# Seeding a PSUM bank by ScalarE in a Strassen-Winograd loop, and copying running sums out in place of VectorE's adds

## The reference

```
y   = x @ W.T + 2 * sum_e gate1[e] * (x @ A[e].T) @ B[e].T      gate1: softmax of the two largest of 8 biased logits
z   = y @ Wf.T + b + 2 * sum_e gate2[e] * (y @ Af[e].T) @ Bm[e]  gate2: softmax over 4 experts
out = x + z
```

## Time and profile before

| | |
|---|---|
| runs | 322.85, 323.37, 323.40 us; median 323.37 |
| profiled execution | span 321.9 us from the first to the last instruction |
| median less that span | 1.5 us |
| TensorE, matmul | 318.2 us busy (99%), 2246 matmuls |
| VectorE | 262.5 us (82%), 609 instructions |
| ScalarE | 128.2 us (40%), 258 instructions |
| GpSimd | 11.3 us (3%) |
| DMA | 27.59 MB |
| granted TensorE clock | 1.000 |

### The profile page before, as it was taken

The page is one execution under the profiler, slowest core; times in us unless marked ns, Lnnn a source line. Parts: engine busy times, 40 slices in busy tenths (PEclk is TensorE's granted clock), DMA queues, the critical chain, the costliest instruction groups (busy, mean ns, idle before and its releaser), DMA issues.

```text
span 321.9 us, 5996 instructions
## 1 busy us (share of the span) xinstructions
PE 318.2 (99%) x2246; PEld 311.9 (97%) x2246; DVE 262.5 (82%) x609; ACT 128.2 (40%) x258; POOL 11.3 (3%) x13
## 2 busy tenths in 40 slices
PE   8999999999999999999999999999999999999996
PEld 5999999999999899899999999999999999999996
DVE  3999999798799778988968968878895987888543
ACT  3872836495147236325412503421251350333111
POOL 1001003700000000000000000000000000000000
DMA  7999000000000312700330150051025006002003
GB/s 266 419 404 290 3 2 0 2 0 2 0 2 0 132 24 46 260 3 0 109 154 1 60 201 0 0 191 70 0 74 187 0 21 239 0 0 110 24 0 130
DMA packets 10704, 27.59 MB, mean 86 GB/s; under 512 B 3166, under 2 KB 4702, under 8 KB 10688
## 3 DMA queue, kind: packets, MB, share of 16 engines
q1 hardware_dynamic: 10256, 26.83, 23.5%
q10 hardware_dynamic: 432, 0.53, 0.5%
HBM read 18.97 MB, written 8.39 MB: 85 GB/s over the span
## 4 chain that ended last, share of the span: by engine, by line
PE 98%; DMA 1%; DVE 0%; issue 0%
PE sums L1310 98%; DMA in<-part 1%; PE sums L1571 0%; DVE rows L1069 0%; DVE b_high L806 0%
## 5 line engine op out<-in xcount | busy, mean ns | idle before, releaser
L1310 PE MATMUL sums<-b_high,a_high 128*128 128x256 f32 (+1 forms) x224 | 45.3, 286 | 0.3 <-DVE b_high L806 0.3
L1310 PE MATMUL sums<-b_low,a_high 128*128 128x256 f32 (+1 forms) x224 | 45.2, 286 | 0.0
L1310 PE MATMUL sums<-b_high,a_low 128*128 128x256 f32 (+1 forms) x224 | 45.0, 286 | 0.0
L1310 PEld LDWEIGHTS sums<-b_high,a_high 128*128 128x128 f32 x224 | 34.7, 189 | 1.0 <-ACT a_high L549 0.8
L1310 PEld LDWEIGHTS sums<-b_low,a_high 128*128 128x128 f32 x224 | 34.7, 189 | 0.0
L1310 PEld LDWEIGHTS sums<-b_high,a_low 128*128 128x128 f32 x224 | 34.6, 188 | 0.0
L1310 PE MATMUL sums<-t_high,s_high 128*128 128x354 f32 x96 | 31.3, 326 | 0.0
L1310 PE MATMUL sums<-t_low,s_high 128*128 128x354 f32 x96 | 31.1, 324 | 0.0
L1310 PE MATMUL sums<-t_high,s_low 128*128 128x354 f32 x96 | 31.1, 324 | 0.0
L1069 DVE TENSOR_TENSOR rows<-sums,rows 128x354 f32<-128x354 f32 x48 | 24.4, 522 | 4.1 <-PE sums L1310 3.4
L1310 PE MATMUL sums<-ct_low,st_high 128*128 128x244 f32 (+1 forms) x80 | 25.6, 320 | 0.0
(11 more groups left out here) (151 smaller groups left out, 845.8 us busy)
## 6 DMA issues: line engine op xcount, KB each, us to landing
stage<-tokens SPq DMA_DIRECT2D x14, 512.0 KB, 4.0
out<-rows SPq DMA_DIRECT2D x14, 512.0 KB, 4.9
in<-part SPq DMA_DIRECT2D x7, 585.0 KB, 8.8
in<-part SPq DMA_DIRECT2D x4, 777.0 KB, 14.0
in<-part SPq DMA_DIRECT2D x4, 265.0 KB, 16.4
rows<-tokens SPq DMA_DIRECT2D x2, 512.0 KB, 13.6
out<-rows SPq DMA_DIRECT2D x3, 192.0 KB, 2.3
c_plain<-gate_proj SPq DMA_DIRECT2D x1, 544.0 KB, 18.0
```

The costliest lines, as they stand in the source:

```text
L1310: return nc.tensor.matmul(out_, lhs, rhs, start=start, stop=stop, skip_group_check=True)
```

## The change

In the loop rounds (pairs 2 to 6, `seeding` and `turning`), and only there:

- product 1 is no longer copied to SBUF. ScalarE waits until bank B is out (its own signal) and copies bank A into bank B (`b_seeded`). Product 6 does not open bank B but accumulates on that copy, and waits for `b_seeded`; product 2 waits for nothing of its own.
- since bank B now holds product 1 + product 6 (+ product 7 ...), U2, U3 and the final sum of bank B are plain ScalarE copies of the bank, in place of three VectorE adds. Each has a place in ScalarE's program: U2 behind the seed, U3 behind the second half of ut_high, the final one behind the copy of bank A.
- product 5 moves from behind product 7 to the place between products 1 and 6.
- pairs 0, 1 and 7 stay as they were, but for the constants that they wait for on `r1_read`, as this is no longer signalled in the loop, and a wait of VectorE for `u2_read` before its last add of bank C.

```diff
--- before.py
+++ after.py
@@ -318,6 +318,7 @@
         p6_done = sem("p6_done")
         p7_done = sem("p7_done")
         r1_read = sem("r1_read")
+        b_seeded = sem("b_seeded")
         u2_read = sem("u2_read")
         u3_read = sem("u3_read")
         r22_read = sem("r22_read")
@@ -696,6 +697,8 @@
 
             def pair(j, first=False, second=False, last=False):
                 steady = not first and not second
+
+                seeding = steady and not last
                 if not first:
                     round_next(j, S4, p3_done)
                 if second:
@@ -721,7 +724,15 @@
                 if not first:
                     act.wait_ge(stored[1], 16 * j)
                 act.wait_ge(p1_done, j + 1)
-                copy(rows[:, 1, wide_at(0)], bank(BANK_A)).then_inc(r1_read, 1)
+                if seeding:
+
+                    act.wait_ge(b_out, j)
+                    copy(bank(BANK_B), bank(BANK_A)).then_inc(b_seeded, 1)
+                    act.wait_ge(stored[0], 16 * j)
+                    act.wait_ge(p6_done, j + 1)
+                    copy(rows[:, 0, wide_at(1)], bank(BANK_B)).then_inc(u2_read, 1)
+                else:
+                    copy(rows[:, 1, wide_at(0)], bank(BANK_A)).then_inc(r1_read, 1)
                 if first:
                     act.wait_ge(t4_made, 1)
                     round_t(T4, C11)
@@ -739,6 +750,8 @@
                 act.wait_ge(u_turned, j + 1)
                 if steady and not last:
                     copy(half_of(ut_high, 1), ut_plain_half(1)).then_inc(ut_high_ready, 1)
+                    act.wait_ge(p7_done, j + 1)
+                    copy(rows[:, 1, wide_at(1)], bank(BANK_B)).then_inc(u3_read, 1)
                 else:
                     copy(ut_high[:, :, :], ut_psum).then_inc(ut_high_ready, 1)
                 if second:
@@ -774,6 +787,9 @@
                     act.wait_ge(stored[0], 16 * j)
                 act.wait_ge(a_done, j + 1)
                 copy(rows[:, 0, wide_at(0)], bank(BANK_A)).then_inc(a_out, 1)
+                if seeding:
+                    act.wait_ge(b_done, j + 1)
+                    copy(rows[:, 1, wide_at(0)], bank(BANK_B)).then_inc(b_out, 1)
                 if first:
                     round_next(j + 1, S2, p6_done)
                     round_next(j + 1, S3, p7_done)
@@ -1196,11 +1212,12 @@
                     add_sums(rows[:, 1, wide_at(1)], bank(BANK_C), rows[:, 1, wide_at(1)]).then_inc(r22_read, 1)
 
 
-                if not first:
-                    dve.wait_ge(stored[0], 16 * j)
-                dve.wait_ge(r1_read, j + 1)
-                dve.wait_ge(p6_done, j + 1)
-                add_sums(rows[:, 0, wide_at(1)], bank(BANK_B), rows[:, 1, wide_at(0)]).then_inc(u2_read, 1)
+                if not turning:
+                    if not first:
+                        dve.wait_ge(stored[0], 16 * j)
+                    dve.wait_ge(r1_read, j - 4 if last else j + 1)
+                    dve.wait_ge(p6_done, j + 1)
+                    add_sums(rows[:, 0, wide_at(1)], bank(BANK_B), rows[:, 1, wide_at(0)]).then_inc(u2_read, 1)
                 if turning:
                     turn_u(j)
 
@@ -1213,7 +1230,6 @@
                 else:
                     low_part(ut_low[:, :, :], ut_psum, ut_high[:, :, :]).then_inc(ut_low_ready, 1)
                 if turning:
-                    add_u3()
                     add_r22()
                 if first:
                     split_t(T4, C11)
@@ -1286,8 +1302,9 @@
                 dve.wait_ge(r22_read, j + 1)
                 dve.wait_ge(d_done, j + 1)
                 add_sums(rows[:, 1, wide_at(1)], bank(BANK_D), rows[:, 1, wide_at(1)]).then_inc(d_out, 1)
-                dve.wait_ge(b_done, j + 1)
-                add_sums(rows[:, 1, wide_at(0)], bank(BANK_B), rows[:, 1, wide_at(0)]).then_inc(b_out, 1)
+                if not turning:
+                    dve.wait_ge(b_done, j + 1)
+                    add_sums(rows[:, 1, wide_at(0)], bank(BANK_B), rows[:, 1, wide_at(0)]).then_inc(b_out, 1)
                 if turning:
                     split_s(j + 1, S3)
                 if not last:
@@ -1295,6 +1312,7 @@
                 if first:
                     split_s(j + 1, S2)
                     split_s(j + 1, S3)
+                dve.wait_ge(u2_read, j + 1)
                 dve.wait_ge(c_done, j + 1)
                 add_sums(rows[:, 0, wide_at(1)], bank(BANK_C), rows[:, 0, wide_at(1)]).then_inc(c_out, 1)
                 assert step[0] == STEPS, step
@@ -1558,10 +1576,15 @@
 
                 if first:
                     pe.wait_ge(t_split, T2 + 1)
+                if turning:
+                    product_5(j)
                 pe.wait_ge(s_split, 4 * j + s_no[S2])
-                if not first:
+                if turning:
+
+                    pe.wait_ge(b_seeded, j - 1)
+                elif not first:
                     pe.wait_ge(b_out, j)
-                of_s(BANK_B, S2, t_high[T2], t_low[T2], True).then_inc(p6_done, 1)
+                of_s(BANK_B, S2, t_high[T2], t_low[T2], not turning).then_inc(p6_done, 1)
                 if first:
                     product_5(j, first=True)
 
@@ -1580,7 +1603,8 @@
                 if not steady:
                     turn_u()
 
-                pe.wait_ge(r1_read, j + 1)
+                if not turning:
+                    pe.wait_ge(r1_read, j - 4 if last else j + 1)
                 if first:
                     pe.wait_ge(cw_split, B21 + 1)
                 of_x(BANK_A, 0, 1, cw_high[B21], cw_low[B21], False).then_inc(p2_done, 1)
@@ -1594,8 +1618,6 @@
                 pe.wait_ge(s_split, 4 * j + s_no[S3])
                 pe.wait_ge(u2_read, j + 1)
                 of_s(BANK_B, S3, t_high[T3], t_low[T3], False).then_inc(p7_done, 1)
-                if turning:
-                    product_5(j)
                 if steady:
                     small_y()
                 lora(BANK_A, 0, 0)
```

## The result

The changed kernel took 324.79 us (median of six runs, 323.89 to 325.18); the kernel before 323.31 us in the same comparison. The ratio is 1.0046, 95% interval 1.0032 to 1.0061: slower by 1.5 us, in an interval of 1.0 to 2.0. The forecast was 325.0 us.

A forecast was written before the change was run, and what follows sets the result against it. TensorE, busy 99%, was taken as the bound, so only its waits count. A stall of +1.9 us less 0.3 us coming back, on 323.37 us, gave 325.0 us; own range 324.4 to 325.9, toward other cases 323.6 to 326.4.

The forecast's parts named there:

- What bounds the kernel: Whole kernel: TensorE is busy 99% of 321.9 us, so only its waits count; ut_low before small_y has no slack.
- The order of the slots: Loop rounds: five product slots still end at 229.57, but product 2 moves one 1.95 us slot later.
- What hangs on product 2: Ahead of small_y: late product 2 delays round_x, ut_high, ut_low and the weight load; 0.38 us in five rounds, +1.9 us.
- Its size: Stall ahead of small_y's weight load: 0.36 to 0.39 us, taken as 0.38, in each of five rounds.
- The seed: ScalarE's copy into bank B before product 6: slack 0.7 us with the signal, product 5 as cover, cost nothing.
- The copies out of the bank: ScalarE's copies of bank B: U2 has 1 us slack before product 7, U3 0.9 us before product 4.
- What comes back: Next tokens' load issued 0.43 us earlier, shrinking the DMA wait ahead of the narrow add: -0.3 us.
- The narrow wait: TensorE's wait at narrow product 3 goes: 0.24 us in the last round, about 0.05 in two others.
- The sum: Whole kernel: +1.9 us stall less 0.3 us gives +1.6 us, so 325.0 us.
- the first (hidden): At small_y's weight load: stall under 0.18 us, so +0.4 us, 323.8 us; chance 0.13.
- The second (a further wait at the seed or at U3): Late seed, or U3 delaying product 4, adds a second TensorE wait: 326.5 to 327 us; chance 0.12.
- The third (TensorE's pitch falls with VectorE's reads): All matmuls: fewer VectorE PSUM reads shorten the pitch by 2 ns, -1.9 us in all, 323.1 us; chance 0.05.

The follow-up runs named there:

- the version without the gap: The changed kernel with ScalarE's round_x moved from ahead of both ut_high halves to behind them; 323.11 us, ratio 0.9998 to the kernel before.

## Why the prediction was right, point by point

- **What bounds the kernel** held: VectorE lost 6.3 us of work, and with the wait taken away again this bought nothing that the medians show (323.11 against 323.21 us); TensorE's waits decide. That ut_low had next to no slack before was borne out: every delay of it went to TensorE.
- **The order of the slots** held: product 2's last start lies one slot of 1.95 us ahead of product 7's (228.52 and 230.47).
- **What hangs on product 2** held link by link: round_x 0.45 us after product 2's last start (0.44 said), 1.45 us from there to the end of ut_high (1.47 said), 0.32 us to the end of ut_low (0.33), 0.06 us to the weight load (0.08 to 0.11 said). Moving round_x away took the gap out, a copy of 0.20 us added 0.20.
- **Its size was too large**: 0.38 us a round said. The load came 0.32 us late, and only 0.28 of these were lost (27.345 against 27.068 us of the version without the gap, each the mean of four rounds). What I left out is that the first matmul after the wait starts together with its weight load (230.80 both) and not 0.16 us behind it, which wins 0.16; the next start follows after 0.27 us instead of 0.16, which gives 0.11 of it back. So about 0.05 us of the lateness is not lost. Five rounds make 1.4 us and not 1.9.
- **The seed** held: ready at 223.79, product 6's weights are loaded from 224.63, slack 0.84 less the 0.12 us of the release, 0.7 as said. That product 5 is its cover was shown by taking it away: rounds of 28.24 us against 27.35.
- **The copies out of the bank** held: U3 at 230.83; r22 waited 0.58 us for it, and sec behind it still had to wait 0.22 us for small_y. No wait of TensorE belongs to them.
- **What comes back** held in direction, not in size. VectorE's sum ahead of the fourth narrow add waited for the next tokens 0.97 us before and 0.49 after, in the mean of the last four rounds; 0.43 less was said. The narrow wait is in none of the changed kernel's profiles. But the 0.3 us that I took for it belongs to one execution. From pair 1's mixed tails to pair 6's, the kernel before takes 290.34 - 152.74 = 137.60 us and the version without the gap 289.77 - 152.48 = 137.29, which is 0.3 less; the kernel before with only round_x moved takes 290.52 - 153.12 = 137.40, and that leaves 0.1. Either is too little to be told in the medians.
- **The sum**: in the loop the changed kernel takes 291.95 - 153.28 = 138.67 us. That is 1.07 more than the one profile of the kernel before (1.4 - 0.3), and 1.27 more than the kernel before with round_x moved. The medians differ by 1.5 and 1.6 us in the two comparisons, with intervals from 1.0 and 0.9 us up. The forecast of 1.6 had its largest term 0.5 us too high, so that it lies this near the medians is in part luck. The other 0.2 to 0.5 us can be scatter of the first part, where the mean starts of the loop are 0.3 us apart, but this was not settled.
- **The rivals**: the first (hidden) fell with the five gaps. The second (a further wait at the seed or at U3) did not come; it needs product 5 out of its place. The third (TensorE's pitch falls with VectorE's reads) fell: with fifteen reads fewer the rounds without a gap are 27.07 us, those of the kernel before 27.04 to 27.11 except for its last. The figure of the Trainium skill (TensorE: Matmul & The Clock Gate, Back-to-back issue gap) stays short of the trace in all runs: 0.162 us measured against an estimated 0.150.

## What to carry to other kernels

When products are reordered to cover one wait, list everything that is released by each product that becomes later, on every engine, and what stands behind it in that engine's program: here a rounding that only the next pair wants stood ahead of the one thing TensorE needed next. Moving it behind took two lines, and the whole loss was gone. And an offload from an engine that is not the bound bought nothing here by itself, but it was what made another order possible: the same order cost 8.1 us with the add left on VectorE, and nothing that shows with it gone and round_x moved.

## What was not expected of the hardware

- A weight load that came late cost 0.04 to 0.05 us less than its lateness, however late it was in three kernels: 0.32 us late lost 0.28 a round (27.345 against 27.068 us), 0.52 late lost 0.48 (27.545), 1.22 late lost 1.17 (28.235, product 5 back).
- ScalarE's copy of 354 columns from bank to bank takes 442 ns. Copies of this size from a bank to SBUF are 466 ns in the mean of 26, which looks like a gain by the destination, as the Trainium skill has it (ScalarE: Activation LUTs, Step-by-step: what each stage is for: a destination in PSUM is the faster one). But the SBUF copy that stood in the same place, directly behind pair_exp, took 445 ns. In the same place, then, the trace shows a gain of 3 ns. The SBUF copies before which ScalarE waited take 467 to 471 ns, and two that stood directly behind another instruction 457 and 458; why these two are slower than the one behind pair_exp is open.
